# Gated linear attention with a feed-forward: the attention matrix with its chunks innermost, and level products on alternating banks

## What is computed

```python
g = jax.nn.log_sigmoid(x @ gk_w1 @ gk_w2 + gk_b) / 16.0
S = exp(g_t)[:, None] * S + k_t[:, None] * v_t[None, :]
o_t = q_t @ S
o = o * rsqrt(mean(o * o) + 1e-5) * rms_w
return (o * silu(x @ Wg)) @ Wo
```

## Time and profile before

| | us |
|---|---|
| three executions | 1315.83, 1313.88, 1315.18 |
| median | 1315.18 |
| profiled execution | 1313.97 |
| its span, first to last instruction | 1312.2 |
| mean granted TensorE clock | 0.988 of full speed |

### The profile page before, as it was taken

How to read it: one execution, slowest core, us unless ns; L and a number is a source line. 1 busy time by engine, 2 the same in 40 slices (tenths; PEclk the granted TensorE clock), 3 DMA queues, 4 the chain that set the end, 5 groups by cost and what they waited for, 6 DMA issues and landing times. The chain is left out here.

```text
span 1312.2 us, 23418 instructions
## 1 busy us (share of the span) xinstructions
PE 1230.2 (94%) x8372; PEld 1073.7 (82%) x8372; DVE 1044.8 (80%) x2404; ACT 711.3 (54%) x1443; POOL 635.0 (48%) x893
## 2 busy tenths in 40 slices
PE   5889999999999999999999999999999999999957
PEld 3677889888897888889888788988889888897956
DVE  3769788796978979787787978879697896978863
ACT  5365555656456465644756555565545646465423
POOL 5436353563445544564435635356354554456431
PEclk9989999999999999999999999999999999999988
DMA  3110010100101001010011001010010100100000
GB/s 97 38 33 17 17 49 1 54 17 17 49 21 49 1 17 49 21 49 1 17 49 53 16 17 49 1 54 16 17 49 21 48 2 17 49 21 33 1 17 17
DMA packets 31778, 38.27 MB, mean 29 GB/s; under 512 B 2448, under 2 KB 29104, under 8 KB 31664
## 3 DMA queue, kind: packets, MB, share of 16 engines
q1 hardware_dynamic: 31136, 36.25, 8.3%
q10 hardware_dynamic: 528, 0.52, 0.1%
HBM read 28.38 MB, written 8.39 MB: 28 GB/s over the span
## 5 line engine op out<-in xcount | busy, mean ns | idle before, releaser
L1047 POOL TENSOR_TENSOR k_decayed<-k_decayed,block_totals 128x256 f32<-128x256 f32 x192 | 168.2, 876 | 277.1 <-PE ps_level L298 276.6
L298 PEld LDWEIGHTS ps_level<-q_blockdiag,k_decayed 128*128 128x128 f32 x1792 | 227.1, 191 | 51.5 <-DVE q_blockdiag L585 41.1
L298 PE MATMUL ps_level<-q_blockdiag,k_decayed 128*128 128x128 f32 x1792 | 241.1, 278 | 26.4 <-DVE q_blockdiag L585 25.1
L575 DVE COPY_PREDICATED attn_T<-level_masks,ps_level 128x512 f32<-128x512 uint32 x160 | 152.7, 954 | 16.0 <-PE ps_level L298 16.0
L585 DVE TENSOR_TENSOR q_blockdiag<-q_blockdiag,block_totals 128x512 f32<-128x512 f32 x192 | 141.3, 736 | 28.1 <-PE ps_level L298 28.1
L1053 POOL TENSOR_TENSOR rstd<-rstd,minus_half 128x1 f32<-128x1 f32 x192 | 111.7, 584 | 106.6 <-DVE rstd L636 106.6
L255 PE MATMUL ps_big<-w_ff_hi,h_hi 128*128 128x256 f32 x512 | 150.1, 293 | 3.0 <-DVE h_lo L590 3.0
L257 PE MATMUL ps_big<-w_ff_hi,h_lo 128*128 128x256 f32 x512 | 144.8, 283 | 0.0
L256 PE MATMUL ps_big<-w_ff_lo,h_hi 128*128 128x256 f32 x512 | 144.7, 283 | 0.0
L837 ACT ACTIVATE gelu_out<-ps_big,ff_b_cols 128x512 f32<-128x512 f32 x128 | 88.0, 688 | 79.8 <-PE ps_big L257 43.2
L623 DVE SCALAR_TENSOR_TENSOR o<-o,o_rstd,out_gate 128x128 f32<-128x128 f32 x256 | 93.3, 426 | 45.0 <-POOL o_rstd L1068 45.0
(11 more groups left out here) (113 smaller groups left out, 3155.1 us busy)
## 6 DMA issues: line engine op xcount, KB each, us to landing
w_raw<-L_ffn_w SPq DMA_DIRECT2D x16, 1024.0 KB, 5.6
out<-y SPq DMA_DIRECT2D x16, 512.0 KB, 2.9
x_in<-L_attn_x SPq DMA_DIRECT2D x15, 512.0 KB, 3.9
ff_b_rows<-L_ffn_b SPq DMA_DIRECT2D x8, 128.0 KB, 2.6
x_in<-L_attn_x ACTq DMA_DIRECT2D x1, 512.0 KB, 4.0
w_raw<-L_attn_Wv SPq DMA_DIRECT2D x1, 512.0 KB, 6.0
w_raw<-L_attn_Wg SPq DMA_DIRECT2D x1, 512.0 KB, 7.1
y<-L_attn_Wo SPq DMA_DIRECT2D x1, 512.0 KB, 8.1
```

The source lines that it names most:

```text
L298: last = nc.tensor.matmul(PL[tl][:, c * CH:(c + 1) * CH], kk[:, tl, c * CH:(c + 1) * CH], q[:, :, :, 1, :], start=True, stop=True)
L575: nc.vector.copy_predicated(dst, m.to_broadcast([P, 2 * NCH, HC // h, h]), src)\
L1047: nc.gpsimd.tensor_tensor(k, k, t.to_broadcast([P, n, h]), ALU.mult)\
```

## The change

`Am` gets the axes tile, head pair, query, chunk: the four chunks are innermost. The masked copies, ScalarE's blocks and the attention products get matching access patterns. Odd levels go to ps_out and ps_state instead of the ps_level pair (`LVB`), with the waits that this needs. The diagonal goes through the ps_transpose banks, and its sums come ahead of level 0, its transpose at step 1. On VectorE the query update of a step comes first and the masked copy of a step one step later, behind the feed-forward's `xT_lo`. ScalarE's blocks wait for all masked copies. GpSimd's `weight_lo(1, ...)` moves from steps 1 to 4 to steps 5 to 8.

```diff
--- before.py
+++ after.py
@@ -68,7 +68,7 @@
         qk = sb("q_times_k", [P, KT, T])
         gn = qk
         tot = sb("block_totals", [P, KT, T])
-        Am = sb("attn_T", [P, KT, NCH * 2, CH])
+        Am = sb("attn_T", [P, KT, 2, CH, NCH])
         kT = sb("k_tokens", [P, NCH, D])
         S = sb("state", [P, KT, HV])
         v = sb("v", [P, NCH, DV])
@@ -106,6 +106,7 @@
         PT = [ps(f"ps_transpose{j}") for j in range(2)]
         PL = [ps(f"ps_level{j}") for j in range(2)]
         PO, PS = ps("ps_out"), ps("ps_state")
+        LVB = [PL, [PO, PS]]
 
 
 
@@ -281,40 +282,49 @@
                         if tl == 0:
                             pe.wait_ge(sem["ac_qb"], at("ac_qb", s, 2 * KT))
                             pe.wait_ge(sem["dv_q"], at("dv_q", s, 2 * KT))
-                            if C:
-                                pe.wait_ge(sem["dv_o"], at("dv_o", p, NCH * H))
                             pe.wait_ge(sem["ac_k"], at("ac_k", s, KT))
                         if C:
                             pe.wait_ge(sem["dv_t"], at("dv_t", p, 3 + tl))
                     else:
                         pe.wait_ge(sem["dv_qu"], at("dv_qu", s, 2 * (i - 1) + tl + 1))
                         pe.wait_ge(sem["po_ku"], at("po_ku", s, 2 * (i - 1) + tl + 1))
-                        if i - 1 < MASKED:
-                            pe.wait_ge(sem["dv_cp"], at("dv_cp", s, 2 * (i - 1) + tl + 1))
-                        else:
-                            pe.wait_ge(sem["ac_cp"], at("ac_cp", s, 2 * tl + 2))
+                        if i >= 2:
+                            pe.wait_ge(sem["dv_cp"], at("dv_cp", s, 2 * (i - 2) + tl + 1))
+                        elif C and tl == 0:
+                            pe.wait_ge(sem["dv_o"], at("dv_o", p, NCH * H))
+                        elif C:
+                            pe.wait_ge(sem["dv_st"], at("dv_st", p, states(NCH - 1)))
                     for c in range(NCH):
                         q = qbd[:, tl, :, c * CH:(c + 1) * CH].rearrange("p a (n t h) -> p a n t h", t=2, h=h)
-                        last = nc.tensor.matmul(PL[tl][:, c * CH:(c + 1) * CH],
+                        last = nc.tensor.matmul(LVB[i % 2][tl][:, c * CH:(c + 1) * CH],
                                                 kk[:, tl, c * CH:(c + 1) * CH], q[:, :, :, 1, :],
                                                 start=True, stop=True)
                     last.then_inc(sem["pe_lv"], 1)
 
                 def diag_rows():
 
+                    if C:
+                        pe.wait_ge(sem["dv_oglo"], at("dv_oglo", p, NCH - 1))
+                    else:
+                        pe.wait_ge(c_ready, 3)
+                    pe.wait_ge(sem["dv_q"], at("dv_q", s, 2 * KT - 1))
                     for tl in range(KT):
                         for c in range(NCH):
-                            last = nc.tensor.matmul(PO[32 * c:32 * (c + 1), 0:CH], ind[:, tl, :],
+                            last = nc.tensor.matmul(PT[0][32 * c:32 * (c + 1), 0:CH], ind[:, tl, :],
                                                     qk[:, tl, c * CH:(c + 1) * CH], start=(tl == 0), stop=(tl == KT - 1))
                     last.then_inc(sem["pe_drow"], 1)
 
                 def diag_columns():
                     pe.wait_ge(sem["ac_dg"], at("ac_dg", s, 1))
-                    nc.tensor.transpose(PO[:, CH:2 * CH], o[:, 0, 0:CH], ident[:, :]).then_inc(sem["pe_diag"], 1)
+                    if C:
+                        pe.wait_ge(sem["dv_oglo"], at("dv_oglo", p, NCH))
+                    nc.tensor.transpose(PT[1][:, 0:CH], o[:, 0, 0:CH], ident[:, :]).then_inc(sem["pe_diag"], 1)
 
                 def x3t(kt):
                     pe.wait_ge(sem["dv_xh3"], at("dv_xh3", p, NCH))
                     pe.wait_ge(sem["dv_oglo"], at("dv_oglo", p, 3 + kt))
+                    if B and kt:
+                        pe.wait_ge(sem["dv_dg"], at("dv_dg", s, 1))
                     transpose_tokens(xh, kt).then_inc(sem["pe_x3t"], 1)
 
                 def f1(m):
@@ -420,6 +430,7 @@
                 def st(c):
 
                     pe.wait_ge(sem["ac_kt"], at("ac_kt", s, c // 2 + 1))
+                    pe.wait_ge(sem["ac_cp"], at("ac_cp", s, 6))
                     pe.wait_ge(sem["ac_v"], at("ac_v", s, c + 1))
                     if c:
                         pe.wait_ge(sem["dv_st"], at("dv_st", s, states(c)))
@@ -446,7 +457,7 @@
                     for hd in range(H):
                         tl, hh = hd // 2, hd % 2
                         w = slice(hd * HV, (hd + 1) * HV)
-                        last = nc.tensor.matmul(PO[:, w], Am[:, tl, 2 * c + hh, :], v[:, c, w],
+                        last = nc.tensor.matmul(PO[:, w], Am[:, tl, hh, :, c], v[:, c, w],
                                                 start=True, stop=(c == 0))
                         if c:
                             last = nc.tensor.matmul(PO[:, w], qbd[:, tl, hh, c * CH:(c + 1) * CH],
@@ -476,10 +487,10 @@
 
                 for step in range(2 * NL):
                     if B:
+                        if step == 0:
+                            diag_rows()
                         level(step // 2, step % 2)
                         if step == 1:
-                            diag_rows()
-                        if step == 3:
                             diag_columns()
                     if C:
                         if step == 1:
@@ -569,10 +580,12 @@
 
                     h = LV[i]
                     dve.wait_ge(sem["pe_lv"], at("pe_lv", s, 2 * i + tl + 1))
-                    dst = Am[:, tl, :, :].rearrange("p a (n t h) -> p a n t h", t=2, h=h)[:, :, :, 1, :]
-                    src = PL[tl][:, :].rearrange("p (a n h) -> p a n h", a=2 * NCH, h=h)
-                    m = masks[:, i, :].bitcast(U32).rearrange("p (a n h) -> p a n h", a=1, h=h)
-                    nc.vector.copy_predicated(dst, m.to_broadcast([P, 2 * NCH, HC // h, h]), src)\
+                    if i + tl:
+                        dve.wait_ge(sem["dv_cp"], at("dv_cp", s, 2 * i + tl))
+                    dst = Am[:, tl, :, :, :].rearrange("p a (n t h) c -> p a n t h c", t=2, h=h)[:, :, :, 1, :, :]
+                    src = LVB[i % 2][tl][:, :].rearrange("p (c a n h) -> p a n h c", c=NCH, a=2, h=h)
+                    m = masks[:, i, :].bitcast(U32).rearrange("p (c a n h) -> p a n h c", c=1, a=1, h=h)
+                    nc.vector.copy_predicated(dst, m.to_broadcast([P, 2, HC // h, h, NCH]), src)\
                         .then_inc(sem["dv_cp"], 1)
 
                 def q_update(i, tl):
@@ -715,19 +728,20 @@
                 if C:
                     ln3(3, p)
                 for step in range(2 * NL):
-                    if B and step == 4:
-                        dve.wait_ge(sem["pe_diag"], at("pe_diag", s, 1))
-                        nc.vector.tensor_copy(dg[:, :].rearrange("p (c h) -> p c h", h=H),
-                                              PO[:, CH:2 * CH].rearrange("p (c r) -> p c r", r=32)[:, :, 0:H])\
-                            .then_inc(sem["dv_dg"], 1)
                     if B:
-                        if step // 2 < MASKED:
-                            copy_pairs(step // 2, step % 2)
                         q_update(step // 2, step % 2)
+                        if step == 1:
+                            dve.wait_ge(sem["pe_diag"], at("pe_diag", s, 1))
+                            nc.vector.tensor_copy(dg[:, :].rearrange("p (c h) -> p c h", h=H),
+                                                  PT[1][:, 0:CH].rearrange("p (c r) -> p c r", r=32)[:, :, 0:H])\
+                                .then_inc(sem["dv_dg"], 1)
                     if C:
                         if step == 1:
                             for kt in range(KT):
                                 lo_part(xT_lo[:, kt, :], xT_hi[:, kt, :], PT[kt][:, :], "ac_x3hi", p, kt + 1, "dv_x3lo")
+                    if B and 1 <= step <= 2 * MASKED:
+                        copy_pairs((step - 1) // 2, (step - 1) % 2)
+                    if C:
                         if 4 <= step < 4 + FT:
                             h_lo_part(step - 4)
                         if 12 <= step < 14:
@@ -851,10 +865,11 @@
 
                     h = LV[i]
                     act.wait_ge(sem["pe_lv"], at("pe_lv", s, 2 * i + tl + 1))
+                    act.wait_ge(sem["dv_cp"], at("dv_cp", s, 2 * MASKED))
                     for b in range(HC // h):
                         r = slice(2 * h * b, 2 * h * b + h)
-                        copy(Am[r, tl, :, 2 * h * b + h:2 * h * (b + 1)],
-                             PL[tl][r, :].rearrange("p (a n h) -> p a n h", a=2 * NCH, h=h)[:, :, b, :], "ac_cp")
+                        copy(Am[r, tl, :, 2 * h * b + h:2 * h * (b + 1), :].rearrange("p a h c -> p c a h"),
+                             LVB[i % 2][tl][r, :].rearrange("p (c a n h) -> p c a n h", c=NCH, a=2, h=h)[:, :, :, b, :], "ac_cp")
 
                 def squares(c):
```

(8 more changed lines are left out.)

## The result

The changed kernel takes 1376.26 us (median of 4, 1375.38 to 1377.22) against 1315.27 before: 1.0466 times, 95% interval 1.0447 to 1.0484, 61 us slower. The forecast was 1298, with a range that ends past its 1335 for long masked copies. Of the two mechanisms that it gave the slower side, strided weight loads at 1354 with a chance of 0.18 is the one that happened, and a second, smaller loss stood in its own sum as a gain.

What follows compares the result with a forecast made beforehand. TensorE, 94% busy, was the bound, VectorE second. Gains of 6.1 (seven odd sequences), 1.8 (last), 6.65 (seven even) and 2.4 (sequence 0) made 17.0 us, giving 1298; likeliest case 1290 to 1306, full range reaching past 1335.

Steps and rivals of the forecast that it cites:

- 1335 for long masked copies: Rival: strided PSUM reads keep all ten masked copies per sequence at 1.3 us; 1335 us, chance 0.12.
- strided weight loads: Rival: attention products load attn_T at half speed with 16 bytes between neighbours; +56 us, 1354 in all, chance 0.18.
- The choice of 0 for the weight loads: Attention products' loads of attn_T: bounds 0 and 56 us, taken as 0 because the load may already run at half rate.
- The masked copies: VectorE: four copies per sequence fall from 1.3 to 0.7 us through longer write runs, saving 2.4 us per sequence.
- The early waits: TensorE's level products waiting for VectorE's query update: 25.1 us in 42 places over 15 sequences.
- The early schedule: Sequence 9 reworked: levels (1,0) and (2,0) start at 4.4 and 7.8 us, putting TensorE 1.8 us ahead.
- The last h_lo: VectorE's last input to the first feed-forward-2 tile: TensorE waits 1.4 us in odd sequences; in even ones it is on time.
- +0.87: Net gain in us per odd sequence, after the longer wait for the last h_lo; seven odd sequences give 6.1.
- the sum kept 1.8: Sequence 15: without statistics in step 10, it keeps the full early gain of 1.8 us.
- lands just when wanted: Even sequences: VectorE's 1.8 us per step fits into 2.27, so its last h_lo does not delay TensorE.
- the 0.95: Gain in us per even sequence, from level (2,0) starting at 664.6 instead of 665.58; seven give 6.65.
- Sequence 0: First sequence, with no feed-forward beside it, runs at VectorE's pace and saves the masked copies' 2.4 us.

Runs made afterwards that it cites:

- the ladder: Kernel before the change, with attention products of chunks 0 to 3 loading attn_T at 8, 12, 16 and 28 bytes between neighbours; 1341.44 us, run once.

## Why the prediction was wrong

- **The choice of 0 for the weight loads failed.** The upper bound was near (56 us; measured 61.6, of which 9.0 are hidden in a wait that goes), and so was the finding that load and product are matched at 111 ns with no slack. What failed is the argument for 0, "a half rate may be what it has now": 0.87 ns per column is not a rate that already pays for strides. With 8 bytes it stays, with 16 the load takes 128 ns more. The step from a rate to its cause had no row, while the rule against it stood in the next paragraph. That rule (the Trainium skill, Advanced Engine Details and Errata, SBUF Cachelines: 16-byte lines, two hits needed) is borne out by 196, 257, 320 and 319 ns; the Trainium skill's sentence in SBUF — State Buffer (Door 1: The DMA port swizzle, the note on cachelines) that four fp32 are free is not, since a distance of four fp32 is exactly where the price is full.
- **The masked copies were right**: all at 0.70 to 0.75, 2.4 us less of VectorE per sequence. Reading PSUM with 512 bytes between neighbours cost VectorE nothing; that rival is out.
- **What the copies alone are worth was missed.** The early waits were put down to the order of VectorE and the banks. The layout alone took 21 of the 25 us away. The prediction worked out layout and order together and priced neither alone; so it did not see that beside the layout the new order has 4 us of early waits left to save and brings 8.1 of its own.
- **The early schedule was right** to 0.2 us in the levels, the wait of x3t(1) included. The wait for the diagonal's transpose was 0.20 and not 0.6, as the two levels before it took 0.2 longer and ScalarE was 0.1 sooner.
- **The last h_lo was off twice.** In odd sequences it was forecast 28.8 us after t = 0 and landed at 29.3; TensorE stood there for 2.2 us and not 1.4, as it arrived 0.3 sooner and the h_lo came 0.4 later. That left +0.4 instead of +0.87. The fall of the clock behind this stop, 1.5 us for each odd sequence, was not in the sum at all, and turned it into -1.2. For sequence 15 the sum kept 1.8, as it has no statistics; it has the same stop of 2.17 and the same fall. The step that failed there is that gelu(7) may wait behind ScalarE's blocks because its h_lo "comes later for VectorE's own backlog": VectorE had to wait for it, 0.31 us in the other odd sequences and 1.62 in this one.
- **In even sequences "lands just when wanted" failed.** The 1.8 us per step of VectorE left out what the prediction itself charges for GpSimd's key update: the query update took 1.11 beside it, so a step takes 2.25 of the 2.27 us and the statistics have no room. ScalarE's blocks, costed at nothing, take twice as long and hold the h_lo longer still. TensorE stops for 0.65, and 0.18 of the 0.95 is left.
- **Sequence 0** gave 1 us at the end of its levels, and 0.6 at its first attention product, instead of 2.4. Query and key updates meet at every step there, as VectorE's now comes first; that this is what holds it is argued from their lengths, not tried.

## What to carry over

An access pattern belongs to every reader and writer of a tile: a layout that makes the writer fast has to be priced at the reader that sits on the bound, and here a float32 stationary operand wants neighbours within 8 bytes. Where a row can't decide between a free and a full price on the busiest engine, the test is one kernel with a ladder of distances. And if two edits attack the same wait, price each alone first: the second may find little left to win and still brings its own new waits. Where two chains end at the same time, taking one away shows nothing; a stage that lacks one of them, as the last sequence does here, tells them apart without a new kernel.

## What the runs showed of the hardware

- Loads of 128 float32 columns: 193 ns at 4 bytes between elements, 196 at 8, 257 at 12, 320 at 16, 319 at 28. Products that follow each other were 0.118, 0.172, 0.230 and 0.225 us apart in the ladder, against 0.112 at 4 bytes.
- A masked copy of 512 elements takes 1.3 us with runs of one or two float32 in the destination and 0.7 with four or more; a source in PSUM with 512 bytes between neighbours changes nothing.
- ScalarE's copy from PSUM to attn_T rose from 0.37 to 0.62 us (256 elements) and from 0.59 to 1.12 (512) with 16 bytes between the elements it writes; with 8 bytes it was 0.39 and 0.64.
- A stop of TensorE of 2.2 us was followed by 3.4 us at 1.2 GHz in each of eight sequences; stops at the same place of 1.3 us (split back at steps 1 to 4) and 1.4 us (old layout) were not.
